# A two-layer graph network: a rewritten setup on all 128 rows, and a new layout of the sums over destinations

## What is computed

```python
s, v = x[:, :64], x[:, 64:].reshape(n, 32, 3)
h_s, h_v = s @ lin1_ws * a, einsum('nci,cd->ndi', v, lin1_wv) * a
w = silu(edge_attr_64 @ fc_w1) @ fc_w2
w1, w2, w3, w4, w5 = split(w, [64, 128, 160, 192])      # widths 64, 64, 32, 32, 32
es, ev = h_s[src], h_v[src]
e0, e1 = edge_attr[:, :1], edge_attr[:, 1:4]
m_s1, m_s2 = w1 * es * e0, w4 * einsum('eci,ei->ec', ev, e1)
m_v1, m_v2 = (w2 * es)[:, :, None] * e1, w3 * ev * e0
m_v3 = w5 * cross(ev, e1)
agg = segment_sum(concat(m...), dst) ; out = gates(agg @ lin2 * a + sc(x))
x = layernorm(x + out)
```

## Time and profile before

| what | us |
|---|---|
| time, three runs | 4458.25, 4457.3, 4451.7 (median 4457.3) |
| profiled execution, its time | 4453.04 |
| its span | 4451.0 |
| setup, to its barrier at 134.4; first gather of layer 0 | 138.02 |
| edges of layer 0, last gather | 2098.1 |
| nodes of layer 0 | 2109.9 to 2336 |
| edges of layer 1, first and last gather | 2338.41, 4298.6 |
| nodes of layer 1 | 4312.4 to 4451 |

### The profile page before, as it was taken

The page is one execution under the profiler, slowest core; times in us unless marked ns, Lnnn a source line. Parts: engine busy times, 40 slices in busy tenths (PEclk is TensorE's granted clock), DMA queues, the critical chain, the costliest instruction groups (busy, mean ns, idle before and its releaser), DMA issues. The chain is left out here.

```text
span 4451.0 us, 166762 instructions
## 1 busy us (share of the span) xinstructions
PE 4044.4 (91%) x58000; PEld 3053.2 (69%) x58001; DVE 2847.8 (64%) x7746; ACT 2961.5 (67%) x12216; POOL 3054.0 (69%) x3215
## 2 busy tenths in 40 slices
PE   7888888888888888888979999999999999999987
PEld 4677777777777777776756766666666666666666
DVE  4544444444444444444667888888888888888878
ACT  1566666666666666665337877777777777777753
POOL 2577777777777777776017777777777777777751
PEclk9999999999999999999889999999999999999995
DMA  4222222222222222223334444444444444444433
GB/s 107 71 72 73 72 72 72 72 73 73 72 73 73 72 72 72 72 73 68 104 98 129 121 120 120 122 121 120 121 121 121 121 121 121 122 121 121 121 100 94
DMA packets 356348, 430.11 MB, mean 97 GB/s; under 512 B 203298, under 2 KB 248648, under 8 KB 356112
## 3 DMA queue, kind: packets, MB, share of 16 engines
q0 software_dynamic: 156288, 329.79, 27.4%
q1 hardware_dynamic: 199618, 98.11, 8.2%
q10 hardware_dynamic: 400, 1.68, 0.1%
HBM read 405.56 MB, written 23.74 MB: 96 GB/s over the span
## 5 line engine op out<-in xcount | busy, mean ns | idle before, releaser
L415 POOL DMA_INDIRECT e_rows<-scratch_table,e_index x3136 | 2967.3, 946 | 1010.5 <-issue 926.2
L438 ACT ACTIVATE e_match<-e_match,e_attr 128x40 f32<-128x40 f32 x10976 | 2480.9, 315 | 176.3 <-DMA e_attr<-in_edge_attr 172.1
L470 PEld LDWEIGHTS e_sum<-e_match,e_msg 128*64 128x64 f32 (+1 forms) x50176 | 1714.0, 125 | 698.3 <-DVE e_msg L629 244.3
L470 PE MATMUL e_sum<-e_match,e_msg 128*64 128x40 f32 (+2 forms) x50176 | 1846.2, 223 | 247.5 <-DVE e_msg L626 194.6
L461 PE MATMUL e_w<-k_fc,e_hidden 100*128 100x192 f32 (+1 forms) x4704 | 1275.2, 407 | 0.0
L618 DVE TENSOR_TENSOR e_msg<-e_w,e_rows 128x512 f32<-128x512 f32 x784 | 537.8, 686 | 1008.1 <-DMA e_rows<-scratch_table,e_index 980.0
L461 PEld LDWEIGHTS e_w<-k_fc,e_hidden 100*128 100x128 f32 (+1 forms) x4704 | 833.0, 190 | 385.3 <-issue 364.8
L431 ACT ACTIVATE e_hidden<-e_h 100x512 f32<-100x512 f32 (+1 forms) x784 | 384.4, 490 | 925.9 <-PE e_h L450 921.2
L450 PE MATMUL e_h<-e_inputs,k_fc 128*100 128x512 f32 (+1 forms) x1568 | 708.6, 534 | 57.9 <-DMA e_inputs<-in_inputs 27.0
L608 DVE TENSOR_TENSOR e_misc<-e_misc,e_rows 128x384 f32<-128x384 f32 x392 | 221.8, 566 | 354.2 <-DMA e_rows<-scratch_table,e_index 354.1
L624 DVE TENSOR_TENSOR e_msg<-e_w,e_rows 128x384 f32<-128x384 f32 x784 | 428.1, 546 | 0.0
(11 more groups left out here) (122 smaller groups left out, 1454.0 us busy)
## 6 DMA issues: line engine op xcount, KB each, us to landing
e_rows<-scratch_table,e_index POOLq DMA_INDIRECT x3136
e_inputs<-in_inputs SPq DMA_DIRECT2D x196, 256.0 KB
e_attr<-in_edge_attr SPq DMA_DIRECT2D x392, 24.0 KB, 1.7
e_inputs<-in_inputs SPq DMA_DIRECT2D x196, 40.0 KB
e_index<-in_src SPq DMA_DIRECT2D x392, 4.0 KB
scratch_self<-m_h SPq DMA_DIRECT2D x10, 480.0 KB, 4.5
f_self<-scratch_self POOLq DMA_DIRECT2D x10, 480.0 KB, 5.0
m_xrow<-in_x POOLq DMA_DIRECT2D x10, 400.0 KB, 5.0
```

The lines of the kernel that those rows point to most:

```text
L415: pool.indirect_dma_start(out=rows[j][:, t, :], out_offset=None, in_=table_dram, in_offset=bass.IndirectOffsetOnAxis(ap=index[q][:, c:c + ...
L438: last = nc.scalar.activation(match[j][:, t, c, :], match[j][:, t, 4, :], ACT.Copy, scale=attr[q][:, e0 + t, e:e + 1])
L470: return nc.tensor.matmul(out[rows, c0:c0 + n, :], m[:, t, f:f + rows.stop - rows.start], m5[:, t, which:which + n, :], start=(first and t ...
```

## The change

The setup is written anew. `x` is loaded whole into two tensors of 128 rows that GpSimd has cleared, in five chunks of rising size (0, 2, 6, 14, 30, 50 tiles), so that both products of a tile use all 128 rows. TensorE begins with 24 products of the identity matrix by itself, then runs the 50 tiles with six PSUM buffers for the products and four for `part_a`. VectorE's work on the groups lies between node tiles; the running sum is replaced by one small product with a triangular matrix; ScalarE scales the weights; `sums` is cleared in eight pieces; the relative destinations and the first indices stay in SBUF. In the edge phase of layer 1 the cross product is no longer made by VectorE: both of its terms are messages of their own (`MW` is 512), taken into the sums with their sign by products. The sums go to four chunks in both layers. `edge_weights` of layer 1 uses 64-row products. Both node phases have products that fit the new layout, `table1` has rows of 160, and GpSimd clears all four chunks between the layers.

```diff
-MW = 448
+MW = 512
@@ setup_phase
-        ps_node = [ctx.enter_context(nc.psum_tensor(f"s_psn{i}", [P, 512], F32)) for i in range(2)]
+        CHUNKS = (0, 2, 6, 14, 30, NT)
+        STORES = (0, 5, 10, 15, 20, 25, 30, 35, 40, 45, 48, NT)
+        x_v, x_s = sb("s_xv", [P, NPAD]), sb("s_xs", [P, NPAD])
+        ps_node = [ctx.enter_context(nc.psum_tensor(f"s_psn{b}", [P, 512], F32)) for b in range(6)]
...
+            def clear(c):
+                cols = slice(CHUNKS[c] * P, CHUNKS[c + 1] * P)
+                nc.gpsimd.memset(x_v[:, cols], 0.0)
+                nc.gpsimd.memset(x_s[:, cols], 0.0).then_inc(padded, 1)
...
-            nc.gpsimd.memset(sums[:, :, :], 0.0)
+            for c in range(PIECES):
+                nc.gpsimd.memset(sums[:, :, c * step:(c + 1) * step], 0.0)
...
+            for c in range(24):
+                nc.tensor.matmul(ps_out[:, 0:P], w["ident"][:, :], w["ident"][:, :], start=True, stop=True)
+            pe.wait_ge(node_in, 32)
...
+            def project(n):
+                if n in CHUNKS:
+                    pe.wait_ge(x_in[CHUNKS.index(n)], 32)
+                at_least(pe, h_ready, n - 5)
...
+            for n in range(NT):
+                add_c(n)
+                if n == 11:
+                    lowest()
+                if n == 15:
+                    highest()
...
+                if n == 37:
+                    relative()
@@ edge_phase
-                    c0, n = u * layer.tiles_per_product * WPITCH, w[f"fc2_{L}"].shape[1]
-                    last = nc.tensor.matmul(ps_w[j % 2][:, c0:c0 + n], hidden[j % 2][:, u * P:(u + 1) * P], w[f"fc2_{L}"][:, :],
-                                            start=True, stop=True)
+                    for h in range(layer.tiles_per_product):
+                        c0, k = (u + 2 * h) * WPITCH, fc2.shape[0] // layer.tiles_per_product
+                        last = nc.tensor.matmul(ps_w[j % 2][:, c0:c0 + n], hidden[j % 2][k * h:k * h + k, u * P:(u + 1) * P],
+                                                fc2[k * h:k * h + k, :], start=True, stop=True)
...
+            def wide_sums(out, m, m5, opens, closes):
+
+                product(out, slice(0, 64), 0, m, 64, m5, 0, n=3, start=opens)
+                product(out, slice(0, 64), 3, m, 0, m5, 3, stop=closes)
+
+            def narrow_sums(out, m, m5, opens, closes):
+
+                low, high = slice(64, 96), slice(96, 128)
+                product(out, low, 0, m, 128, m5, 3, start=opens)
+                product(out, high, 3, m, 224, m5, 0, start=opens)
+                product(out, low, 1, m, 160, m5, 3)
+                if L == 0:
+                    product(out, high, 3, m, 256, m5, 1)
+                    product(out, low, 2, m, 192, m5, 3, stop=closes)
+                    return product(out, high, 3, m, 288, m5, 2, stop=closes)
...
+                product(out, low, 3, m, 288, m5, 2, stop=closes)
+                return product(out, high, 2, m, 192, m5, 3, stop=closes)
...
-                    nc.vector.tensor_tensor(comps(cross_a), e3(3), comps(r[:, :, 96:192]), ALU.mult)
-                    nc.vector.tensor_tensor(comps(cross_b[:, :, :]), e3(2), comps(r[:, :, 128:224]), ALU.mult).then_inc(crossed, 1)
...
-                    last = nc.vector.tensor_tensor(comps(m[:, :, 320:416]), w_v(192), comps(m[:, :, 320:416]), ALU.mult)
+                    nc.vector.tensor_tensor(comps(m[:, :, 320:416]), w_v(192), comps(r[:, :, 64:160]), ALU.mult)
+                    last = nc.vector.tensor_tensor(comps(m[:, :, 416:512]), w_v(224), comps(r[:, :, 64:160]), ALU.mult)
@@ layer0_nodes_phase
-            nc.gpsimd.memset(sums[:, 0:3, :], 0.0)
+            nc.gpsimd.memset(sums[:, :, :], 0.0)
...
-                sp.dma_start(rows("table1")[:, :, D:D + 2 * V], h1[s][:, :, 0:2 * V]).then_inc(stored[s], 16)
```

More of the change, by code:

```diff
@@ L149, in setup_phase @@
+        rel_made, made = sem("rel_made"), sem("made")
         block = ctx.enter_context(nc.Block())
@@ L226, in _ @@
+            act.wait_ge(scaled, len(SCALES))
+            act.wait_ge(out0_scaled, 1)
         @block.tensor
         def _(pe):
-            pe.wait_ge(l_in, 32)
-            for c in range(16):
-                vec = c not in (6, 7, 14, 15)
-                col = OUT0_COLUMNS[c] + (64 if c >= 12 else 0)
-                n = V if vec else S
-                last = nc.tensor.matmul(ps_out[:, col:col + n], l2[:, c, :], l3[:, S:S + V] if vec else l3[:, 0:S],
-                                        start=True, stop=True)
```

538 lines of the change are left out of this document (281 added, 257 removed).

## The result

The changed kernel takes 4485.4 us (median of 4, 4483.41 to 4485.89), the kernel before 4457.77 (median of 4). The ratio is 1.0064, 95% interval 1.0047 to 1.0082: slower, where 4368.4 us were forecast. The profiled execution took 4483.41 us with a span of 4481.8.

| stretch | before | after | change | forecast |
|---|---|---|---|---|
| start to first gather of layer 0 | 138.0 | 59.6 | -78.4 | -88.9 |
| gathers of layer 0 | 1960.1 | 1963.5 | +3.4 | 0 |
| last gather of layer 0 to first of layer 1 | 240.3 | 326.6 | +86.3 | 0 |
| gathers of layer 1 | 1960.2 | 1976.2 | +16.0 | 0 |
| last gather to the end | 152.4 | 155.9 | +3.5 | 0 |

The account below looks back on a forecast made before the run. Gathers were taken to bound the edge phases at 5.005 us a group, while the setup hides behind nothing: 4453.0 - 88.9 + 5.4 - 3.4 - 2.0 = 4364.1, plus 4.3 for the median, 4368.4 us; range 4345 to 4470.

Parts of the forecast that it names:

- 49.1 forecast: Setup: first gather of layer 0 at 49.1 us against 138.0 before, a gain of 88.9 us.
- 41.9 was forecast: Setup: VectorE's 19 us of node work and 9.5 of group work, starting 0.9 after the tiles, end at 41.9.
- 3.7 + 3.5 = 7.2: Setup's end: last store lands 3.7 us after VectorE's work, then 3.5 from the barrier to the first gather.
- rival A: Setup stays slow: clock not granted (+25) or VectorE stands beside GpSimd's clearing (up to 20); 4388 to 4394 us; chance 0.14.
- The 10.3 us set for the identity products: Setup: 24 products of 128 columns at the slow clock take 10.3 us, so the first tile starts at 12.5.
- Three small products for wide ones help nothing, VectorE paces the tile.: Nodes of layer 0: smaller products on PE neither gain nor lose time, since VectorE sets the pace; no term.
- +5.4 - 3.4 - 2.0: Nodes of layer 0: longer GpSimd clearing +5.4 us, shorter VectorE wait on stores -3.4, first indices loaded beforehand -2.0.
- rival B: Edge phases: mode changes or the wide part put PE up to 0.23 us a group over the pace; 4370 to 4458; chance 0.10.
- 0.54 + 0.91 + 1.40 + 1.86 = 4.71: Layer 1 edges, PE's us a group: hidden product, edge weights, 64-wide sums, 32-wide sums with turn; under 5.005, so 0 change.
- The two disputed readings: Layer 1 edges: row halves run side by side (weights 0.91, not 1.81); column halves too (32-wide sums 1.76, not 2.64).
- a pace of 5.005: Edge phases: four gathers at 1.251 us each set 5.005 us a group, whatever the row size.
- Rival C: Edge phases: column halves not both at full speed, PE 5.59 us a group, 4690 us, 4597 with layer 1 alone; chance 0.21.

Follow-up runs that it names:

- e3: Changed kernel with the setup's lowest-destination cut done by scalar_tensor_tensor and its group work at later node tiles; 8233.64 us on a slow chip.
- e17: Changed kernel with two added 192-column products a tile in layer 0's nodes, scalar_tensor_tensor cut and late setup group work; 4394.75 us, 0.9884 of kernel before.
- e8: Changed kernel without the 24 identity products at the start; 4480.4 us, 1.0077 of the kernel before on the same chip.
- e5: Changed kernel with two added 192-column products a node tile in the nodes of layer 0, usual chip; 4398.23 us, 0.9889 of the kernel before.
- e2: Kernel before with layer 0's three output-weight products replaced by the changed kernel's four smaller ones, result not the reference's; 7631.17 us, 1.0126, slow chip.
- e1: Changed kernel with two added 192-column products a node tile in the nodes of layer 0, on a slow chip; 8156.87 us.
- e16: Changed kernel with the added 192-column products, and two of twelve 32-wide products a tile left out in layer 1 (result not the reference's); 4380.54 us.
- e7: Changed kernel with late setup group work, added 192-column products, TensorE's loop body doubled, and two added 256-column products a tile in layer 1's nodes; 4838.17 us.
- e6: Changed kernel with two bodies of four groups in one turn of TensorE's loop, both layers; 4832.38 us, 1.0867 of the kernel before.

## Why the prediction was wrong, step by step

**The setup.** 49.1 forecast, 59.6 measured, and the 10.5 between them is the sum of two errors that partly cancel. VectorE's work ended at 56.8 where 41.9 was forecast, 14.9 late; from there to the first gather it took 2.8 where 3.7 + 3.5 = 7.2 were set. That the second was too long softened the first by luck. PE's part held: tiles 0.55 apart, first tile at 11.01 (12.5 forecast). The step that failed was to let VectorE's work on the groups be free beside the clearing; I had it as half of rival A, worth up to 20 us. The stop is 12.2 us long, with PE waiting 10.46. e3 and e17 show that it was the one kind of operation that stood still in the earlier trace rows too. Without it only 5.3 and 3.1 us were won (55.0 against 60.3, 57.1 against 60.2), since a wait of 5.65 and 5.83 us for the stores of the table, which the chain did not have either, takes its place. The 10.3 us set for the identity products was no cost of theirs: they took 8.05, and with them left out PE waits until 11.74 for its weights, the clock rises in the sixth tile, and nothing is lost (e8).

**The nodes of layer 0** are the failed step: "Three small products for wide ones help nothing, VectorE paces the tile." VectorE paced the tile only at the clock that PE had. The earlier trace rows held both levels, and I used them for the setup alone. The rows would have told more: at the slow clock PE's work of a tile is longer than VectorE's (it had no gap in the early rows), and the products that the change makes small are the ones that stream most. That the clock depends on what PE does was weighed in rival A for the setup ("the array has no gap between products now"), and not asked of the stage in which the change takes streaming away. Its price: +86.3 measured, where the sum had +5.4 - 3.4 - 2.0 = 0. None of the three small terms explains it. The clearing grew as forecast, 21.56 us for 16.19. The first gather came 0.70 us after the barrier, 2.37 before, so 1.7 less (2.0 forecast). VectorE's wait on stores went from 17.1 us to nothing here, where PE is late, and to 4.9 in e5 (3.4 less forecast). e2 shows that the small products alone do it, e1 and e5 that it is undone by streaming more.

**Layer 1** is rival B, at +16 where it had up to 90. PE's cycle was forecast as 0.54 + 0.91 + 1.40 + 1.86 = 4.71 and measured as 0.63 + 1.07 + 3.25 = 4.95. The sums were right to 0.02 in each part: the first 32-wide pass starts at 3007.97, so that the 64-wide part took 1.41 (1.40 forecast) and the 32-wide part 1.84 (1.86). The two disputed readings held as well: halves of the columns and halves of the rows run side by side. What was missing is 0.25 us for the changes between full rows and half rows, 0.09 at the hidden product and 0.16 at the edge weights; the forecast had named it, without a term. It is a difference, and no run changes it alone, but the weight loads show where it lies: the first load for half rows starts at 3005.49 with its own pass, where the kernel before has the load for the edge weights at 3002.04, beside the hidden pass ahead of it. The Trainium skill, "TensorEngine Tiling (Array Packing)", Key Properties, says that a change of tiling mode drains the engine; the trace agrees, with this 0.25 us a group. And a whole term was missing: the loop's jump, 0.40 us once in four groups. I had taken the cycle from a group without a jump; where PE has slack no jump is seen in the end of the phase. 4.95 + 0.10 = 5.05 against a pace of 5.005, times 391, are some 18 us, where 16.0 were measured; e16 shows that PE's cycle is what makes them.

**Rival C** had 0.21 of the chance and did not happen. 96 narrow passes take 1.84 us, two of them (one of each half) every 36 ns. The rule of the Trainium skill, "TensorE: Matmul & The Clock Gate", section "Wait — 56ns, not 53.3ns?", of at least about 25 ns between starts, is not broken within one half (36 ns), but does not hold over the two halves together, whose passes start 6 to 7 ns apart.

**Layer 0 and the end** grew by 3.4 and 3.5 us. The gathers of layer 0 were 1.2530 us apart where they had been 1.2508; e5, e8, e16 and e17 have the same layer 0 and 1958 to 1959 us for it, so the 3.4 differ from one execution or chip to the next and were not put down to the change. The 3.5 at the end stayed untested; the granted clock from the last gather to the end was 0.56 there, and 0.61 in the kernel before.

The faster side had been given 0.76 and the slower 0.21, nearly all of it for rival C. The slower side came without C, by a mechanism that no rival named. The range missed by 15 us.

## What to carry to other kernels

Work taken from TensorE can cost time: before making products smaller in a stage whose clock is not always granted, read the clock by windows there and ask what the stage would take at the low level; if PE is then the bound, keep the columns or add idle ones, and measure, since a like addition did harm in another stage (e7). Take a loop's cycle over a whole turn, with its jump and with each change of the array's row mode, before comparing it to a pace that is 5% away. A loop written out twice can be loaded again in every turn, as in e6, and the page's line of the instruction queue tells at once.

## What the runs showed of the hardware

- Two products of 192 columns more a node tile made the stage between the layers 75 to 84 us shorter (326.5 to 251.7, 336.5 to 252.4), with the granted clock at 0.90 for 0.51; two of 32 columns made it 44 us longer (336.5 to 380.1), at 0.53.
- Half-row products (64 rows, two at once on the upper and lower half) cost 1.07 us for 2048 columns in eight passes, where full rows took 1.70 for 1920. Passes on two halves of the columns start 6 to 7 ns apart, and the passes of one half every 36 ns, at 40 columns each.
- A tensor_scalar of 98 by 4 numbers took 12.20 us beside GpSimd's memsets, through the ends of four pieces of them; scalar_tensor_tensor took 0.16 beside the same ones, as did tensor_scalar once they were over.
- Doubling the body of TensorE's loop raised the instruction traffic from 0.38 to 9.88 MB, nearly all of it in layer 1, and the time from the 4485.4 us of the changed kernel to 4832.38, 7.7%.
- On some chips all kernels here take 1.7 to 1.9 times as long. PE waits within a group there, as the timeline of e1 in layer 0 shows, and GpSimd waits 3689.3 us in all for indices (us, times):

```profile
3008.32 0.29 PE L515 MATMUL e_sum<-e_match,e_msg 128*32 128x40 f32 x5 [0.48 <-issue]
3009.75 0.36 PE L515 MATMUL e_sum<-e_match,e_msg 128*32 128x40 f32 x5 [1.13 <-issue]
...
  DMA k_index<-in_src: 3689.3, 365
```

The change costs far more there (layer 1 4275 to 4305 us against 3628 with the old edge phase). It has 206,020 instructions where 166,762 were, which would fit, but no run tests it. Why those chips are late was not found.
